# The rows of tile t+2 are turned behind the down product, next to the activations of tile t

## What is computed

```python
flat_idx = top_k_index.reshape(-1)          # 8 of 32 experts per token
sort_idx = jnp.argsort(flat_idx)
xs = jnp.repeat(x, K, axis=0)[sort_idx]
group_sizes = jnp.bincount(flat_idx, length=E).astype(jnp.int32)
gate = jax.lax.ragged_dot(xs, w_gate, group_sizes)
up = jax.lax.ragged_dot(xs, w_up, group_sizes)
down = jax.lax.ragged_dot(jax.nn.silu(gate) * up, w_down, group_sizes)
unsort = jnp.argsort(sort_idx)
routed = (down[unsort].reshape(T, K, H) * tkw[..., None]).sum(axis=1)
shared = jax.nn.silu(x @ sw_gate) * (x @ sw_up) @ sw_down
return (routed + shared).reshape(hidden_states.shape)
```

## Time and profile before

| | us |
|---|---|
| median of 3 runs | 13,304.63 |
| the profiled execution | 13,301.22 |
| its span, first to last instruction | 13,299.4 |
| PE busy | 12,585.9 |
| DVE busy | 4,435.6 |
| POOL busy | 2,837.1 |
| ACT busy | 2,255.9 |

### The profile page before, as it was taken

One profiled execution on the slowest core, in us unless ns is written; L12 is line 12 of the kernel. 1 busy time (PEld: TensorE's weight loads), 2 busy tenths in 40 slices (PEclk: granted clock), 3 DMA queues, 4 the chain that ended last, 5 costly groups with the idle time before them and its releaser, 6 DMA issues.

```text
span 13299.4 us, 218878 instructions
## 1 busy us (share of the span) xinstructions
PE 12585.9 (95%) x58520; PEld 10224.2 (77%) x58521; DVE 4435.6 (33%) x6772; ACT 2255.9 (17%) x3430; POOL 2837.1 (21%) x2929
## 2 busy tenths in 40 slices
PE   4377799999999999999999999999999999999998
PEld 3333488888888888888888888888888788888887
DVE  8887622222222222222332223223233323222222
ACT  1133211111111111111111112111112212111111
POOL 3222266621111111111111111111111111111111
PEclk7688899999999999999999999999999999999999
DMA  4312222232232332333332324323334434223322
GB/s 187 136 63 76 87 61 60 60 78 59 59 78 60 78 79 59 77 60 79 96 98 59 79 59 110 65 60 96 79 96 115 113 79 115 59 60 71 66 59 53
DMA packets 376393, 1057.82 MB, mean 80 GB/s; under 512 B 142082, under 2 KB 142530, under 8 KB 352552
## 3 DMA queue, kind: packets, MB, share of 16 engines
q0 software_dynamic: 205600, 689.56, 24.9%
q1 hardware_dynamic: 170760, 367.91, 7.5%
HBM read 608.87 MB, written 448.41 MB: 79 GB/s over the span
## 4 chain that ended last, share of the span: by engine, by line
PE 86%; DMA 1%; DVE 0%; issue 0%; ACT 0%; DVEq 0%; SPq 0%; ACTq 0%; POOL 0%; POOLq 0%
PE pg L1409 9%; PE pg L1411 9%; PE pd L1411 9%; PE pd L1410 9%; PE pg L1410 9%; PE pd L1409 9%; PE pu L1411 9%; PE pu L1410 9%; PE pu L1409 9%; PE tx L1404 4%; PE ta L1445 2%; DMA stage<-in_w_all 0%; DVE w_lo L1321 0%; ACT w_hi L1255 0%; DVEq L1054 0%
## 5 line engine op out<-in xcount | busy, mean ns | idle before, releaser
L1370 DVE TENSOR_TENSOR av<-pu,sg 128x512 f32<-128x512 f32 x656 | 453.8, 692 | 5681.0 <-PE pu L1411 5504.9
L1409 PE MATMUL pg<-w_hi,x_hi 128*128 128x512 f32 x5248 | 2113.7, 403 | 13.0 <-DVE x_lo L1332 13.0
L1409 PE MATMUL pd<-w_hi,a_hi 128*128 128x512 f32 x5248 | 2098.2, 400 | 8.1 <-DVEq L1356 8.0
L1411 PE MATMUL pd<-w_hi,a_lo 128*128 128x512 f32 x5248 | 2057.6, 392 | 0.0
L1411 PE MATMUL pg<-w_hi,x_lo 128*128 128x512 f32 x5248 | 2054.6, 392 | 0.0
L1410 PE MATMUL pd<-w_lo,a_hi 128*128 128x512 f32 x5248 | 2053.5, 391 | 0.0
L1410 PE MATMUL pg<-w_lo,x_hi 128*128 128x512 f32 x5248 | 2046.2, 390 | 0.0
L1411 PE MATMUL pu<-w_hi,x_lo 128*128 128x512 f32 x5248 | 2043.5, 389 | 0.0
L1409 PE MATMUL pu<-w_hi,x_hi 128*128 128x512 f32 x5248 | 2041.5, 389 | 0.0
L1410 PE MATMUL pu<-w_lo,x_hi 128*128 128x512 f32 x5248 | 2041.5, 389 | 0.0
L1214 POOL DMA_INDIRECT out_rows<-y,idx_s x656 | 1046.9, 1596 | 4266.2 <-DVE y L1344 4116.2
(11 more groups left out here) (227 smaller groups left out, 10228.4 us busy)
## 6 DMA issues: line engine op xcount, KB each, us to landing
stage<-in_w_all SPq DMA_DIRECT2D x186, 1024.0 KB, 9.3
xt<-in_x SPq DMA_DIRECT2D x16, 2048.0 KB, 12.9
xn_rows<-xn SPq DMA_DIRECT2D x16, 2048.0 KB, 6.7
base_rows<-bs SPq DMA_DIRECT2D x16, 2048.0 KB, 8.4
base<-base_rows SPq DMA_DIRECT2D x64, 512.0 KB, 5.6
out_rows<-base SPq DMA_DIRECT2D x64, 512.0 KB, 2.7
idx_g<-slot_table SPq DMA_DIRECT2D x658, 1.0 KB, 1.7
xraw<-xn_rows,idx_g POOLq DMA_INDIRECT x658
```

What stands on the lines that cost most here:

```text
L1370: v.tensor_tensor(av[:], pu[:], sg[:], ALU.mult).then_inc(av_ready, 1)
L1409: m(dst, hi, whi[:, cols], start=begin, stop=False)
L1411: return m(dst, lo, whi[:, cols], start=False, stop=end)
```

## The change

In tile t PE now goes from the up product straight to the down product of t-1, and behind it turns the rows of tile **t+2** (not t+1), directly ahead of the four squares of `av`: twelve squares in one group. ACT and DVE make x_hi and x_lo of t+2 at the end of their tile, into the buffer that tile t has just read. Before the first tile the rows of tiles 0 and 1 are turned both, and ACT and DVE do these ahead of the second pair of weights. The buffers, POOL's and SP's programs stay as they are.

```diff
--- before.py
+++ after.py
@@ -1292,8 +1292,6 @@
                         high(run, k)
                 with act.Else():
                     act.sem_inc(act_passed, 1)
-                for h in range(2):
-                    x_high(t + 1, 1 - q, h)
                 with act.If(value_of(act, fresh, t + 1, 1) > 0):
                     run = value_of(act, runs, t + 1, E + SH)
                     act.wait_ge(up_done, t + 1)
@@ -1301,15 +1299,20 @@
                         high(run, k)
                 with act.Else():
                     act.sem_inc(act_passed, 1)
+                for h in range(2):
+                    x_high(t + 2, q, h)
                 act.sem_inc(act_passed, 1)
 
             def rest(t, q):
                 begin(t)
 
-            for k in range(4):
+            for k in range(2):
                 high(0, k)
-            for h in range(2):
-                x_high(0, 0, h)
+            for n in range(2):
+                for h in range(2):
+                    x_high(n, n, h)
+            for k in range(2, 4):
+                high(0, k)
             through(act, act_passed, tile, rest)
 
         @block.vector
@@ -1368,8 +1371,6 @@
                 dve.wait_ge(up_done, t + 1)
                 wait_past(dve, ta_done, t)
                 v.tensor_tensor(av[:], pu[:], sg[:], ALU.mult).then_inc(av_ready, 1)
-                for h in range(2):
-                    x_low(t + 1, 1 - q, h)
                 with dve.If(value_of(dve, fresh, t + 1, 1) > 0):
                     lows(t + 1, (2, 3))
                 with dve.Else():
@@ -1378,6 +1379,8 @@
                 if begun:
                     for h in range(2):
                         scaled(t - 1, 1 - q, h)
+                for h in range(2):
+                    x_low(t + 2, q, h)
 
             def rest(t, q):
                 begin(t)
@@ -1386,10 +1389,11 @@
 
             lows(0, (0, 1), 0)
             dve.sem_inc(gate_weights, 1)
+            for n in range(2):
+                for h in range(2):
+                    x_low(n, n, h)
             lows(0, (2, 3), 0)
             dve.sem_inc(up_weights, 1)
-            for h in range(2):
-                x_low(0, 0, h)
             through(dve, dve_passed, tile, rest)
 
         @block.tensor
@@ -1436,10 +1440,10 @@
                 pe.wait_ge(up_weights, t + 1)
                 wait_past(pe, av_ready, t)
                 hidden(pu, q, 2).then_inc(up_done, 1)
-                for h in range(2):
-                    turn_rows(t + 1, 1 - q, h, ahead_of(t, q))
                 if not (isinstance(t, int) and t == 0):
                     down(t - 1)
+                for h in range(2):
+                    turn_rows(t + 2, q, h, ahead_of(t, q))
                 pe.wait_ge(av_ready, t + 1)
                 for i in range(KI):
                     last = nc.tensor.transpose(ta[:, i], av[:, i * P:(i + 1) * P], ident[:])
@@ -1448,10 +1452,11 @@
             def ahead_of(t, q):
 
 
-                return (t + 1) // 2 if isinstance(t, int) else (t - q) // 2 + q
-
-            turn_rows(0, 0, 0, 0)
-            turn_rows(0, 0, 1, 0)
+                return (t - q) // 2 + 1
+
+            for n in range(2):
+                for h in range(2):
+                    turn_rows(n, n, h, 0)
             through(pe, pe_passed, tile, lambda t, q: down(t - 1))
```

## The result

The changed kernel takes **13,723.9 us** (median of 6 runs, 13,722.8 to 13,733.2), the kernel before 13,295.0 us (6 runs, 13,289.2 to 13,305.2). The ratio is 1.032, with a 95% interval of 1.031 to 1.034. The forecast was 13,735. The profiled execution has a span of 13,723.8 us, 424.4 more than before.

What follows compares the result with a forecast made beforehand. PE, busy 95% of the span, was taken to bound the kernel. Squares -26, gather waits +124 and +162, refill +18, clock +153 and prologue -3 made +428: about 13,735 us, +3.2%, range 13,560 to 13,860.

Steps and rivals of the forecast that it cites:

- The squares: On PE in each of 656 tiles: one group of twelve squares saves 0.04 us, -26 us in all, bounds -85 and +59.
- The waits of the first 64 tiles: While the slot table is scattered, gathers land 4.0 us late for PE in every second tile: 31 times, +124 us.
- The expert changes: At 30 changes of expert, the gather lands 5.4 us late for PE amid weight loads: +162 us.
- rival D: Closely following experts wait longer: half of the 30 changes at 10 us for 5.4, +70, 13,805 us; chance 0.12.
- The refill and the clock: Behind each of 61 PE waits: 0.3 us for the first square, +18, and 2.5 us for a clock fall, +153.
- The prologue: Before the first tile: turning tiles 0 and 1 first, x_lo ahead of the second w_lo pair, saves about 3 us once.
- B: The waits come but PE's clock holds behind them: 13,580 us; chance 0.18.
- C: A wait in every tile of the scatter stage, not every second: 31 more, +211, so 13,945 us; chance 0.08.
- E: Gathers are in time, POOL's chain being shorter than 17.7 us: 13,275 us, or 13,215 by the squares' bound; chance 0.05.

Runs made afterwards that it cites:

- two scatters early: Changed kernel with two of each tile's eight scatters put ahead of the add and six behind it, in the first 64 tiles: 13,586.5 us.
- y_last: Changed kernel with VectorE's two x_lo of tile t+2 put back ahead of the scaling of y: 14,564.4 us, ratio 1.095.
- the filled runs: 14 unread squares of the unit matrix ahead of the twelve in the first 64 tiles: 13,700.6 us in the changed kernel, 13,620.2 with four scatters early.
- down_loads_held: Changed kernel, but SP issues a new expert's last two weight loads only when the gather has landed: 13,653.9 us, ratio 1.026.
- four_index_buffers: Changed kernel with four idx_s buffers for two, so the index copy waits for the add of four tiles ago: 13,621.1 us, ratio 1.024.
- scatter_halves: Changed kernel with four of each tile's eight scatters put ahead of the add and four behind it, in the first 64 tiles: 13,548.2 us.

## Why the prediction was right

**The squares.** -26 predicted, -28 measured. The middle value held: twelve squares take the 1.23 us that were added up, and one return is saved.

**The waits of the first 64 tiles.** 31 waits of 4.0 us, in every second tile, from a gather priced in the earlier trace rows; the profile has 32 with a mean of 4.1. That neighbouring delays add up to the lateness stood on an argument about what y hangs on. Three runs bear it out: the changed kernel (lateness 4), two scatters early (1.4 over two tiles), and y_last, where the argument's premise is removed and nearly every tile waits. "31 waits" was the form only for a lateness of this size.

**The expert changes.** 30 waits of 5.4 predicted, 34 with a mean of 6.0 measured, 6.4 to 6.9 at a lone change. The step that was short: I took the chain of the earlier trace rows as it stood. In the changed kernel it is 1 us longer from add to gather (12.9 then, 13.8 now; the copy alone takes 1.58 in place of 0.73). The close experts of rival D are there (16.4 us the longest), but few; half of 30 was too many. The longest wait stands in place of the 11.5 us that PE had idled for `av` before, which I had not counted. Both kinds of wait together: 124 + 162 = 286 predicted, 323 more idle time measured.

**The refill and the clock.** 18 + 153 = 171 predicted, 129 left over in the budget: the count was right (61 predicted, 61 falls behind waits), the price was 2.1 us in place of 2.8. No row ahead of the run was named for the refill's 0.3 us; the traces show 0.16 before the first square and some 0.05 within the eight at full clock (1.09 in place of 1.04). The clock's 2.5 I took from products, 14 of them 0.20 late. Here it is mostly twelve squares: 0.9 us for the eight, 0.5 for the four, 0.3 for the first product. And the filled runs say that what the clock alone costs is less still: removing 33 falls gave back 23 us, since 0.75 us of the slower start stays at full clock and the gathers moved later. The Trainium skill, "TensorE: Matmul & The Clock Gate", "HAM oscillation — how this bites in real kernels", has the clock put down anew at each wait for a DMA between bursts of products. The trace agrees at the long waits: all 60 of 3.69 us or more were followed by a fall.

So the two misses, +37 in the waits and -42 behind them, have opposite signs, and that the total is within 11 us is luck. The range did not need it: with either miss alone the time would have been 13,772 or 13,693. The 3 us that the prologue should have saved don't show: the first gate product starts within 1 us of where it did.

**The rivals.** B fell: the clock did fall. C fell, and y_last shows what it would have been. D holds in a few places. E fell at its own point: the chain is some 21.7 us, and the run with half the scatters early is what E looks like in the first 64 tiles.

**The other edits.** The prologue and ACT's new order leave no wait in the list; x_hi stands under PE's tx as before.

## What to carry to other kernels

Moving a consumer two thirds of a period earlier (here 12 of 17.7 us) asks that much of every producer behind it: walk the chain from the last thing that it hangs on (here the end of a down product) round to the consumer and compare it with the period, for each kind of tile apart. A date missed by L costs L over two tiles when the chain starts from work that ran ahead of the wait, and L in each when it starts behind it. A gain of 0.04 us a tile buys nothing if one tile in ten then waits 4 us.

## What the runs showed that I had not expected

- Waits of nearly one length end in either clock. Of 19 waits of 2.03 to 2.37 us in down_loads_held, 8 were followed by a clock of 0.5 and 11 by full clock; two of 2.16 us, one of each, are shown above. In the nine profiles of the changed order with gathers, every wait of 3.7 us or more was followed by a fall and none of 1.8 or less; in between both happen (1.89 fell in four_index_buffers, 3.64 did not in scatter_halves). A length alone doesn't tell it there.
- Behind a short wait PE idles a second time, some 0.45 us ahead of the first product behind the squares. Its read of the plan, which an ordinary tile has behind it by then, ends 0.8 us before that product. In y_last 254 tiles have this second idle time behind a wait, and the distance is 0.77 to 0.82 us in all of them.
- A gather of 512 KB takes 3.9 us from issue to landing alone and 8.6 beside two weight loads of 1 MB; the add takes 9.2 beside four. POOL's copy of 1 KB grew from 0.2 to 0.7 and 1.6 us in such places.
